# The one-hots of node rows in the edge phase of a graph network kernel, by a compare that also writes a row sum

## What is computed

```
h        = silu(edge_rbf @ W1 + b1)                 # 8 attributes of an edge -> 128
weights  = h @ W2 + b2                              # 128 -> 128
messages = node_feats[col] * weights                # col = dst
aggregated = segment_sum(messages, row, n_nodes)    # row = src
combined = concatenate([node_feats @ Wself + bself, aggregated], -1)
x        = layernorm(x + combined @ Wcat + bcat)
```

## Time and profile before

| what | value |
|---|---|
| three executions | 7383.6, 7390.78, 7395.26 us (median 7390.78) |
| the profiled execution, its own time | 7380.97 us |
| its span, first to last instruction | 7379.3 us |
| granted TensorE clock, mean of the span | 0.74 of full |
| busy over the span | POOL 5424.9, PE 4769.2, DVE 3253.6, ACT 1394.4 us |
| edge phase, first scatter to end of the last | 146.6 to 2365.2 us, 2218.6 us |

### The profile page before, as it was taken

How to read it: one execution, slowest core, us unless ns; L and a number is a source line. 1 busy time by engine, 2 the same in 40 slices (tenths; PEclk the granted TensorE clock), 3 DMA queues, 4 the chain that set the end, 5 groups by cost and what they waited for, 6 DMA issues and landing times.

```text
span 7379.3 us, 116998 instructions
## 1 busy us (share of the span) xinstructions
PE 4769.2 (65%) x26801; PEld 4098.6 (56%) x26801; DVE 3253.6 (44%) x7139; ACT 1394.4 (19%) x3899; POOL 5424.9 (74%) x6168
## 2 busy tenths in 40 slices
PE   5999999899997988444444444444555555554447
PEld 4887787787787888343333433334444444444342
DVE  7676676676676777322222422223222222222228
ACT  2333333333332000200000000001111111110007
POOL 2777777777777887677777777777777777777765
PEclk8777877878777999656666666666777777776668
DMA  3333333333334876322222222222333333332225
GB/s 109 117 117 118 116 117 119 115 116 117 113 119 129 240 230 212 93 54 54 53 54 53 51 53 54 53 54 56 75 75 73 73 75 73 73 74 63 53 82 171
DMA packets 963698, 709.01 MB, mean 96 GB/s; under 512 B 608595, under 2 KB 829390, under 8 KB 962946
## 3 DMA queue, kind: packets, MB, share of 16 engines
q0 software_dynamic: 161968, 341.31, 16.1%
q1 hardware_dynamic: 621046, 260.06, 14.5%
q10 hardware_dynamic: 180577, 106.59, 5.0%
HBM read 543.58 MB, written 170.28 MB: 97 GB/s over the span
## 4 chain that ended last, share of the span: by engine, by line
POOL 43%; issue 15%; PE 7%; DVE 2%; ACT 1%; DVEq 0%; POOLq 0%; DMA 0%; SPq 0%; ACTq 0%
POOL arena L825 42%; PE bank L1963 6%; DVE acc_a L1507 1%; ACT acc_a L1015 0%; PE bank L2057 0%; PE bank L2010 0%; DVE arena L1734 0%; DVEq L424 0%; DVE arena L1738 0%; POOL prior L797 0%; POOLq L91 0%; DVE arena L1730 0%; DVE some_mv L1528 0%; POOLq L92 0%; DVE arena L1520 0%
## 5 line engine op out<-in xcount | busy, mean ns | idle before, releaser
L825 POOL DMA_INDIRECT arena<-x1d,edge x3322 | 3151.2, 949 | 1016.8 <-issue 1012.3
L2010 PE MATMUL bank<-arena 128*128 x8320 | 1704.7, 388 | 2167.7 <-SPq L592 1520.7
L2010 PEld LDWEIGHTS bank<-arena 128*128 128x128 f32 x8320 | 1590.0, 294 | 2305.4 <-issue 2298.8
L766 POOL DMA_INDIRECT msgs<-arena x1664 | 1688.1, 1014 | 657.8 <-issue 501.9
L1649 DVE TENSOR_TENSOR arena<-bank,arena 128x1024 f32<-128x1024 f32 x520 | 636.5, 1224 | 3113.4 <-PE bank L2010 3006.8
L1051 ACT ACTIVATE arena<-edge,arena 128x4 f32 x1040 | 223.8, 285 | 2621.1 <-issue 2147.6
L1915 PE MATMUL bank<-w2s,acc_b 128*128 128x128 f32 x3328 | 684.3, 370 | 0.0
L1915 PEld LDWEIGHTS bank<-w2s,acc_b 128*128 128x128 f32 x3328 | 580.8, 263 | 126.1 <-issue 126.1
L1963 PE MATMUL bank<-arena 128*128 128x128 f32 x3712 | 500.4, 293 | 82.2 <-DVE acc_a L1507 53.1
L1898 PE MATMUL bank<-arena 128*128 (+1 forms) x3328 | 552.4, 318 | 1.6 <-DVE arena L1429 1.6
L1400 DVE TENSOR_TENSOR_SCAN acc_b<-arena,acc_b 128x512 f32<-128x512 bf16 x415 | 531.5, 1281 | 7.5
(11 more groups left out here) (318 smaller groups left out, 4303.2 us busy)
## 6 DMA issues: line engine op xcount, KB each, us to landing
arena<-rows SPq DMA_DIRECT2D x208, 512.0 KB
arena<-msgs ACTq DMA_DIRECT2D x464, 136.0 KB, 3.4
arena<-msgs SPq DMA_DIRECT2D x464, 136.0 KB, 3.3
arena<-x1d,edge POOLq DMA_INDIRECT x3322
msgs<-arena POOLq DMA_INDIRECT x1664
pred<-arena ACTq DMA_DIRECT2D x98, 256.0 KB
arena<-pred SPq DMA_DIRECT2D x12, 1792.0 KB, 8.4
arena<-xwin SPq DMA_DIRECT2D x208, 64.0 KB
```

The lines of the kernel that those rows point to most:

```text
L766: pool.indirect_dma_start(msgs, bass.IndirectOffsetOnAxis(ap=pos[:, b, j:j + 1], axis=0), mrow[:, b, j, :], None).then_inc(scattered[b], 16)
L825: pool.indirect_dma_start(grow_t[:, sl, 0:D], None, x1d, bass.IndirectOffsetOnAxis(ap=edge2[:, odd * RING + sl, 1:2].bitcast(i32), axis=0) ...
L2010: last = mm(sum_at(q, u), oh1[:, q % 2, u * UT + k, :], rows[:, k * CW:(k + 1) * CW], start=(k == 0), stop=(k == UT - 1))
```

## The change

The compare of L1429 becomes the form of `tensor_scalar` with a second operation and `accum_out`: it adds 0.0 to each element, which leaves the one-hots as they are, and writes the sum of each partition's 1024 results to a column of a new small tile, `hots_in_row`, one column per buffer half. Nothing reads that tile. Its two words lie in `arena` behind `posf`, so `drow` and `widx` move by two words.

```diff
         posf = cut(2 * TG).rearrange("p (s j) -> p s j", s=2)
+        hots_in_row = cut(2)
         drow = cut(TG * 2).rearrange("p (j c) -> p j c", c=2)
...
                 g = 2 * it + b
                 need(dve, s["xj_ready"], 2 * g - 2)
-                v.tensor_scalar(wsel[:, b], rowsb[:, b, 1, :].rearrange("p (j e) -> p j e", j=TG), iota_c[:, :], None, ALU.is_equal).then_inc(s["wsel_ready"], 1)
+                v.tensor_scalar(wsel[:, b], rowsb[:, b, 1, :].rearrange("p (j e) -> p j e", j=TG), iota_c[:, :], 0.0, ALU.is_equal, ALU.add,
+                                accum_out=hots_in_row[:, b:b + 1]).then_inc(s["wsel_ready"], 1)
```

## The result

The changed kernel takes **7489.6 us** (median of 4 executions, 7485.5 to 7491.7) where the kernel before takes 7393.0 in the same series: a ratio of 1.0132, with a 95% interval of 1.0115 to 1.0150. The forecast was 7321 us. The change is slower by 97 us, and the measured time lies outside the range.

The account below looks back on a forecast made before the run. POOL's scatter queue was taken to bound the edge phase. Scatters freed from the compare gain 75 us, the chain gives back about 6, the start adds 1.3: written as -70, giving 7321 us, range 7290 to 7354.

Parts of the forecast that it names:

- What bounds the kernel: Edge phase: POOL's queue of scatters sets its end, 10.67 us per group, with message halves ready well ahead.
- What a scatter takes: POOL's scatters: 0.962 us undisturbed, mean 1.014; the compare L1429 holds 138 of them, 75 us in all.
- step 4: POOL's scatter queue: the accumulating compare no longer shuts POOL out, so 75 us go and the phase takes 2143 us.
- the remaining 15 us: Edge phase scatters: lengthening next to instructions other than the compare, which may shift with the phases.
- The forecast's rule: VectorE's compare in a two-port mode locks GpSimd out; the accumulating form cannot enter that mode, so 75 us would go.
- Step 1: VectorE's compare: grows from 0.73 us to 1.39 us with a separate small instruction, 137 us more on DVE.
- Step 2: VectorE in the edge phase: 3.2 us idle per group and its lead over POOL hide the longer compare, costed at nothing.
- Step 3: Start of the edge phase: two compares precede the first scatter, +1.3 us.
- Step 5: Message chain of TensorE, ACT and DVE: must follow at 10.30 us per group; its own pace is 10.2 to 10.5.
- The sum: Whole kernel: POOL's gain 75, about 6 given back by the chain, start +1.3, written as -70, giving 7321 us.
- The chain takes over: Rival, edge phase: the message chain binds instead of POOL, gain only 50 to 28 us, 7341 to 7363; chance 0.14.
- The compare still shuts POOL out, and for longer: Rival, scatters: accumulating compare keeps the lock for 1.22 us instead of 0.73, 92 us slower, 7483; chance 0.07.

Follow-up runs that it names:

- e3: Old compare, both hidden halves in one PSUM bank, scans' second input a PSUM column of -1, against the kernel before: 7325.3 us, ratio 0.9920.
- e1: Old compare, one hidden bank, plus a 448-column PSUM copy between compare and mask as delay, against the kernel before: 7482.1 us, ratio 1.0134.
- e9: Kernel before with the old compare moved behind the second scan, no work added: 7550.5 us, ratio 1.0213 to the kernel before.
- e6: Old compare, one hidden bank, running counts placed in PSUM bank 1, against the kernel before: 7305.5 us, ratio 0.9884.
- e4: Changed compare, one hidden bank, scans' second input a PSUM column of -1, against the kernel before: 7331.6 us, ratio 0.9920.
- e7: Changed compare, one hidden bank, running counts placed in PSUM bank 1, against the kernel before: 7299.5 us, ratio 0.9873.
- e11: e7 with the other compare, L1393, in the accumulating form too, against the kernel before: 7288.6 us, ratio 0.9876.
- e2: Changed compare, one hidden bank, plus a 512-column PSUM copy behind the compare as delay, against the kernel before: 7368.8 us, ratio 0.9978.

## Why the prediction was wrong, point by point

**What bounds the kernel** was right: POOL's queue of scatters sets the edge phase in all thirteen traces. The time of each kernel follows its sum of lengthening.

**"What a scatter takes" is the step that failed.** It reads: "So L1429 shuts POOL out of something that a scatter needs in its second half." With it fell the 75 us that step 4 took off POOL's queue: the scans held those scatters, and went on to hold more. The observation under it was sound: all 138 long scatters that overlap the compare end 0.117 to 0.146 us after it. But the compare follows the scan without a gap and always takes 0.73 us, so a scatter that ends 0.12 after the compare also ends 0.77 after the scan. Two candidates with a constant distance can't be told apart by how constant the distance is. The earlier trace rows held a hint: the scatter at 1242.56, 1.01 us with no compare at its side, starts in a mask that ends 0.17 later. The forecast had put that kind down as "the remaining 15 us"., a scatter that starts 0.02 us after the compare and takes 0.96, was explained by a need in the "second half", but does not decide: in e3, where the old compare does hold scatters, the 67 that start so close behind its beginning take 0.96 too. Sorting scatters by what runs at their start, rather than by what overlaps them, points to scan and mask; e1, e3 and e9 then show it.

The forecast's rule is not empty. It holds for scatters that start 0.24 to 0.31 us before the old compare, as e3 and e6 show. In the kernel before these are 21 of the 138, with 2.7 us, and the scan in front would have held them as long by itself. The reading "the trace agrees on the lock" was therefore too strong: in that trace nothing tells the compare's hold from the scan's.

The forecast also rested on the wrong sentence of the right page. The Trainium skill, SBUF — State Buffer, Who interferes with whom, says in the same list that a VectorE instruction with two SBUF inputs contends with a GpSimd instruction that reads SBUF. By that, scan and mask are suspects, and the indirect DMAs read their places from SBUF. The traces agree, with 0.77 and 0.83 us from release to end. The Trainium skill infers in the same list that `tensor_tensor` does not stall the DMAs that GpSimd issues; for these indirect ones the 208 scatters held at a mask speak against that.

**Step 1**, the compare's length: 1.34 us for both instructions against 1.39 taken. VectorE's busy time grew by 106 us where 137 were taken. **Step 2**, that this is hidden on VectorE and that no one waits for it: right as far as waiting goes; POOL waited for messages 22.0 us in 150 to 2460 us instead of 17.4, still 0.3 us at a time, and the median lead over POOL even grew from 7.7 to 8.6 us. But "I cost it at nothing" is the second step that failed. Delay on VectorE was free of waits and still moved the second scan by 0.55 us, so that a scatter started inside it: +78 us at the scans and +25 at the masks, which together are nearly the whole loss. **Step 3**, the start, was nothing: the first scatter began 1.6 us earlier, at 145.0.

**Step 4**, -75 us: the accumulating compare indeed holds no scatter. The changed kernel's own trace hardly tests this, since 69 of its 206 start within 0.03 us of the compare's beginning and 137 in its last 0.11 us; e4, e7 and e11 do, with 398 well inside it and none held. But the old one added nothing to the scan's hold in the kernel before, so there was nothing to win. The lock between the old compare and GpSimd is real, e3 shows it, at 14 us beside it and 3 before it; here it was covered. **Step 5**, the chain that follows at 10.2 to 10.5 us per group: it was never put to the test in the changed kernel, and in e11 it keeps up at 10.24, with VectorE busy 161 us more over the phase than in the changed kernel. The pace of 10.46 was that of one stretch, not a limit. **The sum**: its terms as written give -68 and not -70, which changes nothing here.

**The rivals.** "The chain takes over" did not happen. "The compare still shuts POOL out, and for longer" gave 7483 and came within 7 us of the measurement, for a reason that the traces refute: held scatters end 0.40 us before the compare does, and in e4 others start in it unharmed. Its price counted longer holds at one instruction; what happened is holds at a second one. That was luck. A number that fits is no proof of its mechanism; e1, with the old compare and the same loss, speaks for the other one.

## What to carry to other kernels

Where a queue of equal instructions on GpSimd bounds the time, list for each lengthened one what VectorE was running at its start, and group by that before naming a cause, then change one suspect at a time; a constant distance to an end can belong to any instruction of a fixed chain. Work on VectorE that nobody waits for is not free if it moves an instruction with two SBUF inputs relative to that queue: 0.6 us of added delay cost 1.3% or gained 1.6% here, by where it put the next scan. Better than tuning the distance is to put one of the two inputs into PSUM: with the counts there, 0.5 us of longer compare (e6 to e7) cost nothing.

## What the runs showed of the hardware that was not expected

- An indirect DMA on GpSimd that starts while VectorE runs an instruction with two SBUF inputs is held until that one ends: it ends 0.77 us after a scan and 0.83 us after a multiply, against 0.96 undisturbed. It is not held when it starts 0.05 to 0.07 us after the scan has begun (99 in e2; the scan takes 1.30 to 1.31 us instead of 1.28), nor when the scan has less than 0.19 us left (the 0.96 less the 0.77).
- The same scan of 512 elements with its second input in PSUM takes 1.28 us, and with output in PSUM too 1.29, and does not hold it: 1246 of 1296 that start well inside it are not lengthened, and the other 50 end 0.12 us after the old compare behind it. A mask with one input in PSUM doesn't hold it either (0 of 204 in e6, where 137 of 203 were lengthened in e3).
- The fast compare bf16 to f32 (1024 elements in 0.73 us) holds it as well, when it starts 0.3 us or more into the compare (116 of 116 in e3, 113 of 113 in e6) or 0.24 to 0.31 us before it (22 and 28). The accumulating form (1.25 and 0.08 us) does not: none of 398 well inside it in e4, e7 and e11.
- A held scatter sets the phase of those behind it: it ends 0.77 us after the scan, and the next ones start 1.07 and 2.33 us after the scan's end. So the distance of the next scan decides. The same instructions in another order (e9) took 2.1% more time, and more of them (e2) 0.2% less.
